# Experts' first layer in three fp32r products, with weights split ahead of time by GpSimd

## The reference

```python
xf = x.reshape(-1, DIM)                       # 2048 rows of 256
logits = xf @ gate_w + gate_b
top_w, top_i = jax.lax.top_k(logits, K)       # K = 2 of 8 experts
gw = jax.nn.softmax(top_w, axis=-1)
combine = (gw[:, :, None] * one_hot(top_i, E)).sum(axis=1)
for e in range(E):
    h = gelu(xf @ w1[e] + b1[e])              # 256 -> 1024, the first layer
    out = out + combine[:, e:e + 1] * (h @ w2[e] + b2[e])
shared = gelu(xf @ ws1 + bs1) @ ws2 + bs2
return out + shared
```

## Time and profile before

| | |
|---|---|
| time, median of 3 runs | 807.6 us (804.71 to 807.96) |
| the profiled execution's own time | 804.94 us |
| its span, first to last instruction | 803.2 us |
| granted TensorE clock, mean | 0.971 |
| PE busy | 743.4 us, 93% |
| PEld busy | 565.3 us, 70% |
| DVE busy | 405.7 us, 51% |
| ACT busy | 332.2 us, 41% |
| POOL busy | 218.6 us, 27% |
| DMA | 71.76 MB, mean 89 GB/s |

### The profile page before, as it was taken

The page is one execution under the profiler, slowest core; times in us unless marked ns, Lnnn a source line. Parts: engine busy times, 40 slices in busy tenths (PEclk is TensorE's granted clock), DMA queues, the critical chain, the costliest instruction groups (busy, mean ns, idle before and its releaser), DMA issues. The chain is left out here.

```text
span 803.2 us, 14818 instructions
## 1 busy us (share of the span) xinstructions
PE 743.4 (93%) x4804; PEld 565.3 (70%) x4805; DVE 405.7 (51%) x807; ACT 332.2 (41%) x885; POOL 218.6 (27%) x217
## 2 busy tenths in 40 slices
PE   6689999999999999999999899999999999999960
PEld 5567666967696767669999866767676767676740
DVE  3767788787879776666875321212121212222214
ACT  1232556456636654463332124343434343434324
POOL 5772212151114103002078201212121212122223
PEclk9987999999999999999999999999999999999995
DMA  9952341404050713042133499312121212121116
GB/s 291 248 152 55 54 115 36 86 25 148 0 108 0 226 31 52 7 142 86 57 119 107 98 325 316 75 33 33 33 33 33 33 33 33 33 33 33 27 15 214
DMA packets 60489, 71.76 MB, mean 89 GB/s; under 512 B 15264, under 2 KB 49952, under 8 KB 59552
## 3 DMA queue, kind: packets, MB, share of 16 engines
q1 hardware_dynamic: 47968, 57.03, 25.8%
q0 software_dynamic: 7152, 9.34, 6.9%
q10 hardware_dynamic: 5328, 4.85, 2.2%
HBM read 45.57 MB, written 25.11 MB: 88 GB/s over the span
## 5 line engine op out<-in xcount | busy, mean ns | idle before, releaser
L1829 PE MATMUL ps<-we,hT 128*128 x624 | 142.8, 382 | 2.5 <-ACT hT L815 2.5
L1829 PEld LDWEIGHTS ps<-we,hT 128*128 128x128 f32 x624 | 119.7, 192 | 35.5 <-issue 20.8
L1809 PE MATMUL ps<-we,xT 128*128 x312 | 140.9, 594 | 0.3 <-issue 0.3
L1330 DVE COPY hp<-ps 128x512 f32<-128x512 f32 x78 | 50.3, 686 | 155.1 <-PE ps L1809 155.1
L1103 DVE TENSOR_REDUCE mx<-ps 128x4 f32<-128x512 f32 (+1 forms) x128 | 103.6, 819 | 20.6 <-PE ps L1627 19.4
L815 ACT ACTIVATE hT<-ps,b1T 128x128 f32<-128x128 f32 x312 | 85.0, 383 | 51.4 <-PE ps L1820 51.4
L1809 PEld LDWEIGHTS ps<-we,xT 128*128 128x128 f32 x312 | 56.1, 190 | 56.6 <-issue 56.5
L613 ACT ACTIVATE xT<-ps 128x256 f32<-128x256 f32 x39 | 15.0, 385 | 161.3 <-PE ps L1792 161.3
L726 ACT ACTIVATE pT<-ps 128x256 f32<-128x256 f32 x128 | 49.2, 385 | 69.8 <-PE ps L1643 59.5
L1627 PE MATMUL ps<-k_stack,q_stack 96*128 96x256 f32 (+1 forms) x256 | 72.3, 367 | 5.3 <-DVE mx L1103 3.1
L592 POOL CAST yidx<-meta 128x1 int32<-128x1 f32 x39 | 7.2, 184 | 237.1 <-ACT yw L824 237.1
(11 more groups left out here) (238 smaller groups left out, 1107.9 us busy)
## 6 DMA issues: line engine op xcount, KB each, us to landing
we<-in_w SPq DMA_DIRECT2D x16, 1024.0 KB, 8.9
k_stack<-k_rows SPq DMA_DIRECT2D x24, 256.0 KB, 4.8
slot_rows<-attn SPq DMA_DIRECT2D x1, 4992.0 KB, 23.9
xs<-slot_rows ACTq DMA_DIRECT2D x37, 128.0 KB, 2.0
k_rows<-k_s SPq DMA_DIRECT2D x16, 256.0 KB, 2.1
q_stack<-q_rows SPq DMA_DIRECT2D x48, 64.0 KB, 5.6
x_raw<-in_xT SPq DMA_DIRECT2D x4, 512.0 KB, 5.0
XW<-in_x SPq DMA_DIRECT2D x4, 512.0 KB, 8.3
```

Source lines behind the costliest of these rows:

```text
L1330: last = nc.vector.tensor_copy(hp[:, c * 512:(c + 1) * 512], ps[:, 2 + c, :])
L1809: m = nc.tensor.matmul(ps[:, 2 + c, :], xT[:, q, k, :], w[:, bass.ds(e, 1), k * HID + c * 512:k * HID + (c + 1) * 512].rearrange("p o n -> ...
L1829: m = nc.tensor.matmul(ps[:, 6, 0:D], hT[:, c, :], w[:, bass.ds(e, 1), KD * HID + c * D:KD * HID + (c + 1) * D].rearrange("p o n -> p (o n)"),
```

## The change

The first layer of the experts (`hidden`) is computed with `mm3`. For each tile that is 12 fp32r products of 512 columns in place of the 4 float32 products. The input has two parts: ACT writes the high part of `xT` as it wrote `xT` before, and DVE gets a new step `x_lo` for the low part (a subtraction of 128 x 256 from PSUM).

The weights `w1` are split by POOL during attention. For each of the 8 experts POOL issues the load of 1 MB, makes the high part (`w1_hi`, a copy of 128 x 2048), then the low part (`w1_lo`, a subtraction of 128 x 2048), and issues two stores of 1 MB to `w1_split` in DRAM. Expert 0 is done in the first body, 1 and 2 in the second, 3 and 4 in the third, 5, 6 and 7 in the last. The buffers are those of `v_s`, `pT_s`, `a_s` and `c_s` while attention does not use them, which adds a wait to ACT (`w_saved` before it writes `v_s`) and a wait of POOL for `w1_ps`. `prod` has two pieces in place of four, and `shift_piece` takes each sum one unit behind its product, in units 3 to 6. POOL's loop over the two middle bodies is written out.

In SBUF the split `w1` of four experts fits (`w1r`, a ring; expert e goes to place e modulo 4), and `w2` of all eight (`w2r`). SP loads a pair's `w1` from `w1_split` (2 MB each) and waits, from expert 4 on, until the tiles of expert e-4 are past `hidden` (`tile_end`). The `w2` of experts 0 and 1 are now issued after `w2_ps`, between the early `w1` loads and the load of `b2b`. DVE works out two more tables (`places`) and `tile_end` behind the routing. PE reads three table entries for a tile, and its order for tile t is now: hidden(t+1), turn_x(t+2), output(t), turn_h(t+1). Several semaphores are merged (`consts`, `masks`, `h_ps`) with the same conditions.

The diff, cut to its core:

```diff
+RING = 4
+W2_AT = 2
...
+        w1_split = nc.dram_tensor("w1_split", (E, P, 2, KD * HID), F, kind="Internal").ap()
...
+        stage_a = (raw_a[:, :], pT_s[:, :, :, :].rearrange("p l n q -> p (l n q)")[:, 0:KD * HID],
+                   v_s[:, :, :, :].rearrange("p l n d -> p (l n d)"), 0)
+        stage_b = (raw_b[:, :], c_s[:, :, :, :].rearrange("p l k t -> p (l k t)"),
+                   a_s[:, :, :, :].rearrange("p l k t -> p (l k t)"), 1)
...
-        we = sb("we", [P, E, EW], F, mo)
+        w1r = sb("w1r", [P, RING, 2, KD * HID], FR, mo)
+        w2r = sb("w2r", [P, E, NH * D], F, mo)
...
-            def load_expert(e):
-                sp.dma_start(we[:, e, 0:KD * HID].rearrange("p (k n) -> p k n", k=KD),
-                             w1_d[e].rearrange("(k p) n -> p k n", p=P)).then_inc(s["we_in"], 16)
-                sp.dma_start(we[:, e, KD * HID:].rearrange("p (k n) -> p k n", k=NH),
+            def load_w1(e):
+                sp.dma_start(w1r[:, e % RING, :, :].bitcast(F), w1_split[e]).then_inc(s["we_in"], 16)
+            def load_w2(e):
+                sp.dma_start(w2r[:, (e + W2_AT) % E, :].rearrange("p (k n) -> p k n", k=NH),
                              w2_d[e].rearrange("(k p) n -> p k n", p=P)).then_inc(s["we_in"], 16)
             sp.wait_ge(s["pv_done"], 8 * 2 * B)
+            sp.wait_ge(w_saved[0], 32 * (E - 1))
+            sp.wait_ge(w_saved[1], 32)
...
             for e in range(EARLY):
-                load_expert(e)
+                load_w1(e)
...
+            sp.wait_ge(s["w2_ps"], 2 * B)
+            for e in range(EARLY):
+                load_w2(e)
...
-            sp.wait_ge(s["sy_ps"], CHUNKS)
+            sp.wait_ge(s["h_ps"], 1)
+            sp.wait_ge(s["table_ready"], 1)
             for e in range(EARLY, E):
                 if e % EARLY == 0:
                     sp.wait_ge(s["we_in"], 32 * e)
-                load_expert(e)
+                if e >= RING:
+                    sp.wait_ge(s["h_ps"], sp.value_load(tile_end[0:1, e - RING:e - RING + 1], min_val=1, max_val=TILES + 1))
+                load_w1(e)
+                load_w2(e)
                 if e == EARLY:
                     rows_kept(CHUNKS - 1)
...
+            def w1_load(e, stage, nth, free):
+                for sem_, value in free:
+                    pool.wait_ge(s[sem_], value)
+                if nth:
+                    pool.wait_ge(w_saved[stage[3]], 32 * nth)
+                pool.dma_start(stage[0].rearrange("p (k n) -> p k n", k=KD),
+                               w1_d[e].rearrange("(k p) n -> p k n", p=P)).then_inc(w_raw[stage[3]], 16)
+            def w1_hi(e, stage, nth):
+                pool.wait_ge(w_raw[stage[3]], 16 * nth + 16)
+                nc.gpsimd.tensor_copy(stage[1], stage[0]).then_inc(s["w_split"], 1)
+            def w1_lo(e, stage, nth):
+                pool.wait_ge(s["w_split"], 2 * e + 1)
+                nc.gpsimd.tensor_tensor(stage[2], stage[0], stage[1].bitcast(F), ALU.subtract).then_inc(s["w_split"], 1)
+                pool.dma_start(w1_split[e, :, 0, :], stage[1].bitcast(F)).then_inc(w_saved[stage[3]], 16)
+                pool.wait_ge(s["w_split"], 2 * e + 2)
+                pool.dma_start(w1_split[e, :, 1, :], stage[2].bitcast(F)).then_inc(w_saved[stage[3]], 16)
...
+                late = 7 if last else 2 * b
+                nth = 6 if last else late
+                if not first:
+                    w1_load(2 * b - 1, stage_a, 2 * b - 1, ())
+                    if last:
+                        w1_load(6, stage_b, 0, (("qk2_ps", 4 * B), ("v2_ps", 2 * B)))
                 if not last:
                     split(a_s, x_raw, (("x_raw_in", 16 * b + 32), ("qk2_ps", 4 * b + 4)), "xa_split", b + 1)
                 if not first:
+                    w1_hi(2 * b - 1, stage_a, 2 * b - 1)
+                    w1_lo(2 * b - 1, stage_a, 2 * b - 1)
+                    if last:
+                        w1_hi(6, stage_b, 0)
+                        w1_lo(6, stage_b, 0)
+                        w1_load(late, stage_a, nth, ())
                     pool.wait_ge(s["pv_done"], 8 * 2 * b)
                     pool.wait_ge(s["at_lo"], b)
                 pool.wait_ge(s["v2_out"], 2 * b + 2)
...
                                         .broadcast_to([P, NT, HEADS, DH]), ALU.add)\
                     .then_inc(s["v_set"], 1)
                 if not last:
+                    w1_load(late, stage_a, nth, (("w1_ps", 2 * b + 4),))
                     split(c_s, c_raw, (("v2_ps", 2 * b + 2), ("c_raw_in", 16 * b + 32)), "ctx_split", b + 1)
                 if not first:
                     norm_pow(2 * b, 1)
                     norm_x2(b - 1, 2 * b)
+                w1_hi(late, stage_a, nth)
                 if not last:
                     norm_pow(1 if first else 2 * b + 1, 0)
+                w1_lo(late, stage_a, nth)
...
+                    if g is not None:
+                        act.wait_ge(w_saved[0], 64 * (g + 1))
...
-                    copy(xT[:, q, :, :], ps[:, 7 * q, 0:KD * P].rearrange("p (k t) -> p k t", k=KD), "xT_out")
+                    copy(xT[:, q, 0, :, :], ps[:, 7 * q, 0:KD * P].rearrange("p (k t) -> p k t", k=KD), "xT_out")
...
-                at, t = 9 * n - 10, (u - 2) % NT
+                at = 9 * n - 10
                 if 2 <= u < 2 + NT:
-                    nc.vector.tensor_tensor(prod[:, t, :], X[:, bass.ds(NT * n + t, 1), :].rearrange("p o d -> p (o d)"),
+                    t = u - 2
+                    if t >= 2:
+                        dve.wait_ge(s["shift_step"], at + 2 * t - 1)
+                    nc.vector.tensor_tensor(prod[:, t % 2, :], X[:, bass.ds(NT * n + t, 1), :].rearrange("p o d -> p (o d)"),
                                             u_row[:, :], ALU.mult).then_inc(s["shift_step"], 1)
-                if 6 <= u < 6 + NT:
-                    dve.wait_ge(s["shift_step"], at + t + 1)
-                    nc.vector.tensor_reduce(shift[:, bass.ds(NT * n + t, 1)], prod[:, t, :], AX, ALU.add)\
+                if 3 <= u < 3 + NT:
+                    t = u - 3
+                    dve.wait_ge(s["shift_step"], at + max(2 * t, 1))
+                    nc.vector.tensor_reduce(shift[:, bass.ds(NT * n + t, 1)], prod[:, t % 2, :], AX, ALU.add)\
                         .then_inc(s["shift_step"], 1)
...
+            for i, wrap in enumerate((RING, E - W2_AT)):
+                link(nc.vector.tensor_scalar(tab_s[:, i, :], tab_f[:, :], float(wrap), -float((RING, E)[i]), ALU.is_ge, ALU.mult))
+                nc.vector.scalar_tensor_tensor(out=places[:, i, :], in0=tab_f[:, :], scalar=float((0, W2_AT)[i]),
+                                               in1=tab_s[:, i, :], op0=ALU.add, op1=ALU.add)
+            nc.vector.tensor_scalar(tile_end[:, :], end_e[:, :], 1.0, None, ALU.add).then_inc(s["table_ready"], 1)
...
+                def x_lo(t, q):
+                    dve.wait_ge(s["xT_out"], t + 1)
+                    lo_of(xT[:, q, 1, :, :], ps[:, 7 * q, 0:KD * P].rearrange("p (k t) -> p k t", k=KD),
+                          xT[:, q, 0, :, :], "xT_lo")
...
                         h_out(2 * i + q + 1)
+                        x_lo(2 * i + q + 2, q)
                         y_sum(2 * i + q, q, True)
...
-                def hidden(t, q, e):
-                    pe.wait_ge(s["xT_out"], t + 1)
+                def place(i, t):
+                    return pe.value_load(places[0:1, i, bass.ds(t, 1)], min_val=0, max_val=(RING, E)[i] - 1)
+                def hidden(t, q):
+                    e, at = expert(t), place(0, t)
+                    weights(e)
+                    pe.wait_ge(s["xT_lo"], t + 1)
                     if not (isinstance(t, int) and t == 0):
                         pe.wait_ge(s["h_out"], t)
                     for c in range(2):
                         for k in range(KD):
-                            m = nc.tensor.matmul(
-                                ps[:, 2 + c, :], xT[:, q, k, :],
-                                w[:, bass.ds(e, 1), k * HID + c * 512:k * HID + (c + 1) * 512].rearrange("p o n -> p (o n)"),
-                                start=k == 0, stop=k == KD - 1)
+                            cols = slice(k * HID + c * 512, k * HID + (c + 1) * 512)
+                            m = mm3(pe, ps[:, 2 + c, :], lambda l: xT[:, q, l, k, :],
+                                    lambda l: w1r[:, bass.ds(at, 1), l, cols].rearrange("p o n -> p (o n)"),
+                                    k == 0, k == KD - 1)
...
                 with pe.Fori(1, 1 + LOOPS) as i:
-                    t = 2 * i
-                    e1 = expert(t + 1)
-                    weights(e1)
-                    hidden(t + 1, 1, e1)
-                    output(t, expert(t))
-                    e2 = expert(t + 2)
-                    turn_x(t + 2, 0)
-                    weights(e2)
-                    turn_h(t + 1)
-                    hidden(t + 2, 0, e2)
-                    output(t + 1, e1)
-                    turn_x(t + 3, 1)
```

(28 more changed lines are left out.)

135 lines of the change are left out of this document (69 added, 66 removed).

## The result

The changed kernel takes 829.5 us (median of 4 runs, 817.9 to 837.3) where the kernel before takes 807.6 in the same call: a ratio of 1.022, 95% interval 1.017 to 1.027. A ratio given with an interval leaves out executions more than 1.5% above the fastest of their kernel, so it is not always that of the medians. Run again later, the same kernel gave 831.6 against 806.2, 1.032 (1.028 to 1.037). It is slower, and in the second call the whole interval lies above 2%; the forecast was 796 us, with 12% for slower. The profiled execution took 828.2 us, its span 826.5, 23.3 more than before.

A forecast was written before the change was run, and what follows sets the result against it. PE was taken as the bound in the expert loop and attention. On 804.94 us, −22.6 (loop) + 10 (splits) + 1.5 (routing) + 1 (rest) gave 794.8, or 797.5 on the median; forecast 796, own range 788 to 802, 8 in 10: 783 to 808.

The forecast's parts named there:

- The loop: Expert loop over tiles: `hidden` falls from 3.45 to 2.87 us, the tile to 7.42, a gain of 22.6 us.
- The faster pace of a rival: Expert loop: PE takes 216 ns a product, 12 cost 2.59 us, 33.5 us gained, 785 us in all; chance 0.05.
- `output` keeps 0.22 us behind the gelu: Expert loop: the slack between gelu's end and `output`'s start shrinks from 0.58 to 0.22 us but holds.
- GpSimd's splits beside DVE: Attention, two middle bodies: POOL's split instructions hold DVE's `prod`, 5 us lost per body, 10 us together, bounds 0 and 16.5.
- POOL's own time costs nothing: Attention: the splits' 66 us on POOL cost nothing themselves, since POOL has idle stretches such as 28.5 us ahead of `v_aug`.
- The rule that the prediction cited: Attention: a DVE instruction with two SBUF inputs and a GpSimd instruction reading SBUF contend, and the other fully blocks.
- 10 us for attention: Attention, two middle bodies: the loss of 5 us per body from `prod` held by POOL's splits.
- The saves hold the keys: Rival, three batches behind the first: POOL's stores and load make `k_stack` up to 7 us late, 814 us; chance 0.11.
- Routing: Behind attention: `b2b` lands late behind `w2` loads, DVE is delayed and nothing covers it; 1.5 us lost, bounds 0 and 4.
- the sign given: Routing: PE's wait for `xs` of 3.5 us or more would show the second loss.

The follow-up runs named there:

- before_stall: The kernel before with two extra DVE reductions ahead of the first `res` of each group of four; 846.5 us against 824.4, ratio 1.025.
- No_stores: The changed kernel with both split stores cut to 16 columns and the ring filled from unsplit weights; 839.8 us, ratio 1.014 to the kernel before.
- pieces8: The changed kernel with `w1_hi` and `w1_lo` each in 8 instructions of 256 columns; 851.9 us, ratio 1.031 to the kernel before.
- half_whole2: The changed kernel with only experts 4 to 7 split in attention, at other places, unsliced steps, four-piece `prod`; 794.0 us, ratio 0.978 to the kernel before.
- prod4: The changed kernel with four-piece `prod`, sums in units 6 to 9, middle bodies' first split after the last sum; 814.3 us, ratio 1.010 to before.

## Why the prediction was wrong, point by point

*The loop.* Right. 2.87 us per `hidden` is what was taken, the tile is 7.33 (7.42 forecast; `turn_h` took 0.79 and not 0.87), and the stretch is 26.8 us shorter where 22.6 were forecast. The faster pace of a rival did not show. The forecast that `output` keeps 0.22 us behind the gelu was too low (0.51), and its reason held: ACT's copy comes earlier.

*GpSimd's splits beside DVE: the step that failed.* The prediction looked for the hold only where the trace of before showed it, at `prod`, and took 10 us for two bodies. There the hold was small: `prod` took up to 1.41 us in batch 1 and 1.68 in batch 2 (2.5 to 5 forecast), and PE waited 1.01 us in batch 1 (0.97 before). `x_raw` came late against the products, so that the split of `a_s` held the third and fourth in place of the first two, and the fourth was through before `w1_lo` began. The splits were also shorter than taken, 1.9 to 2.1 and 4.5 to 4.6 us for 3.28 and 4.95. The heavy hold was at `res`, behind `norm_pow`, in three bodies and not two. The order on GpSimd showed it: `w1_lo` stands directly behind the instruction that lets DVE's next step go, so that the two meet in each of these bodies. "POOL's own time costs nothing" held there (GpSimd stood idle ahead of each `norm_pow`), and `norm_pow` was priced by whether it is late, not by what starts with its end.

The rule that the prediction cited is for two inputs in SBUF, and `res` reads one tile; another item of the same section bears on it. The Trainium skill, "SBUF — State Buffer", section "Who interferes with whom", lists `tensor_scalar` among the operations that can take the shared pair of ports, when their operands meet its conditions. The trace agrees with the hold (it does not show the ports): `res` went from 0.40 to 4.57 us beside `w1_lo`, while `mx` beside the next `w1_lo` kept its 0.7 to 1.0 us.

*The price of a wait: failed as well.* The sum counted a wait at its own length. PE's waits of 2.77, 2.75, 2.74 and 3.26 us are new, and all its idle time in the seven halves grew by 12.5 us; the time lost is 33.9 + 12.7 = 46.6. The other 34, by difference, go with the 81.9 us at 1.2 GHz, in which the same products take longer (the third half shows it with no added idle time). In before_stall a wait of 2.99 us cost 4.8; the 3.26 us in the last body cost 3.1 + 12.7. So 10 us for attention were a term mis-sized in two ways: the hold at the wrong step, and the clock left out.

*The saves hold the keys.* This rival, with 0.11 and 814 us, was half right: the place was the last body alone, the wait 3.26 us there, and for `q_stack`. It too had counted PE's waits only. No_stores shows the wait to be the stores'. Ahead of the first halves of batches 1 to 3, pieces8 shows waits of 1.93 to 3.85 us for the keys once DVE's stall is gone, and there it is GpSimd's load that they meet.

*Routing.* 1.5 us forecast. DVE waited 1.03 us for `b2b`, which landed in 9.2 us and not 6.1, and PE waited 1.60 us for DVE in the shared expert, a wait that the trace of before does not have. But PE's wait for `xs` fell from 2.20 to 0.76 (3.5 or more was the sign given), and from the last turning of attention's result (353.34 and 403.71) to the first `turn_x` (452.36 and 503.05) there are 99.0 and 99.3 us. Right as far as DVE's delay, wrong in that nothing would cover it: worth 0.3.

```profile
439.76 0.69 DVE L1297 TENSOR_TENSOR ws<-ps,b2b 128x512 f32<-128x512 f32 x1 [1.03 <-DMA b2b<-in_b]
...
454.75 0.63 PE L1801 MATMUL ps<-ident,XW 128*128 128x128 f32 x4 [1.60 <-DVE xT_s L926]
```

What stays open: why one wait brings 3.4 us at half clock and another 30.7. Waits of 0.8 to 1.4 us were followed by none (before, at 129.24), by 13.7 and 20.5 (the changed kernel) and by 30.7 us (half_whole2); no run here separates the reasons.

## What to carry to other kernels

Before an idle engine is given background work, list what it releases: work that stands right behind a releasing instruction starts together with what was released, and if the two share a path they collide every time. Price a wait of PE not by its length but by its length and the clock behind it; here waits of about 3 us cost 1.6 to 5 times as much, and waits of about 1 us sometimes nothing more and sometimes a fall that cost 5 to 12 us. And when a stall is taken away, look at what it covered: the transfers that had time until then can become the next wait.

## What the runs showed of the hardware that was not expected

A GpSimd instruction of 4.5 us holds a DVE step that reads one SBUF tile and two columns of scalars (0.40 to 4.57 us) that starts with it; in pieces of 256 columns the hold is 0.2 to 0.5 us, and GpSimd's own work grows from 4.52 to 5.75. One wait of PE of 2.99 us, with no transfer or GpSimd work added, was followed by 3.4 us at 1.2 GHz three times out of three. A half with no more idle time of PE than before was 5.5 us longer with the clock at half for 13.7 us. In prod4 one execution lay 9 us above the other four, with a lower mean clock. In the call of before_stall, the shared expert's stage had PE idle with "issue" as the only cause and the clock at half for 17 to 31 us in all four kernels; in the other calls it had not.
